# A macaron network of six parts on one Trainium2 core: gate product and integers on VectorE, another order of loads, a signal of their own for ten more scores

## The reference

```python
x = x + 0.5 * ffn8(_ln(x))      # int8 quantised 128x128 product
x = x + enc(_ln(x))             # gated encoder, see below
x = x + 0.5 * ffn8(_ln(x))
x = x + 0.5 * moe(_ln(x))       # top-2 routing to 8 experts, capacity 256, hidden 688
x = x + attn(_ln(x))            # 16 heads of width 8
x = x + 0.5 * moe(_ln(x))       # the same experts again
# in enc: xl = alpha * (dense @ wv + wvb);  sw = sigmoid(-xl) ** 2
#         xo = xl * 2 * sw + 2 * enc * (1 - sw)
# in ffn8: q = clip(round(lhs / scale), -127, 127); acc = q @ q_rhs; acc * scale * rhs_scale
```

## Time and profile before

| | us |
|---|---|
| median of 3 runs (lowest, highest) | 3003.58 (3001.66, 3004.78) |
| the profiled execution | 3014.93 |
| its span | 3012.6 |
| mean granted TensorE clock | 0.852 |

### The profile page before, as it was taken

One profiled execution on the slowest core, in us unless ns is written; L12 is line 12 of the kernel. 1 busy time (PEld: TensorE's weight loads), 2 busy tenths in 40 slices (PEclk: granted clock), 3 DMA queues, 4 the chain that ended last, 5 costly groups with the idle time before them and its releaser, 6 DMA issues.

```text
span 3012.6 us, 42205 instructions
## 1 busy us (share of the span) xinstructions
PE 2171.7 (72%) x13556; PEld 1596.8 (53%) x13556; DVE 1513.2 (50%) x4298; ACT 1242.2 (41%) x2620; POOL 708.3 (24%) x678
## 2 busy tenths in 40 slices
PE   2666662463983888798878888878988898947845
PEld 1454341343752655675666566646755665725734
DVE  4885673333374365457445554564464355345412
ACT  3675203323354345435534553444444334324312
POOL 2110004242122032332134222422232230022042
PEclk9877755685996899999999999999999999969878
DMA  7000000012012121311131213212121311221011
GB/s 219 1 0 0 1 0 5 21 47 48 28 43 47 40 61 43 73 49 50 41 82 56 54 31 75 58 45 56 53 59 44 79 53 44 45 57 52 18 52 37
DMA packets 228506, 140.34 MB, mean 47 GB/s; under 512 B 117073, under 2 KB 206284, under 8 KB 228306
## 3 DMA queue, kind: packets, MB, share of 16 engines
q1 hardware_dynamic: 173264, 84.55, 11.4%
q0 software_dynamic: 16928, 34.72, 4.0%
q10 hardware_dynamic: 38114, 18.53, 2.1%
HBM read 81.50 MB, written 57.15 MB: 46 GB/s over the span
## 4 chain that ended last, share of the span: by engine, by line
PE 49%; DVE 20%; issue 8%; ACT 7%; POOL 5%; DMA 5%; SPq 3%; ACTq 1%; DVEq 1%; POOLq 0%
PE PS L851 15%; PE PS L819 9%; DVE AR L1012 4%; PE PS L1086 4%; PE PS L1123 4%; PE PS L1104 3%; PE PS L1109 2%; DVE small L322 2%; PE PS L1276 2%; POOL AR L701 2%; PE PS L854 1%; DMA OD<-AR 1%; DVE xnT L1184 1%; DMA YE<-AR 1%; SPq L1167 1%
## 5 line engine op out<-in xcount | busy, mean ns | idle before, releaser
L851 PE MATMUL PS<-AR,W 128*128 128x256 f32 x2560 | 649.6, 403 | 18.4 <-DVE AR L747 13.1
L745 DVE TENSOR_TENSOR AR<-AR,PS 128x512 f32<-128x512 f32 (+1 forms) x384 | 229.2, 598 | 757.7 <-ACT AR L786 625.7
L851 PEld LDWEIGHTS PS<-AR,W 128*128 128x128 f32 x2560 | 500.1, 204 | 92.4 <-DVE AR L747 15.3
L1012 DVE TENSOR_REDUCE AR<-PS 128x2 f32<-128x512 f32 x512 | 344.5, 690 | 274.1 <-PE PS L1109 227.3
L786 ACT ACTIVATE AR<-PS 128x512 f32<-128x512 f32 (+1 forms) x384 | 201.5, 526 | 667.4 <-PE PS L851 520.5
L690 POOL DMA_INDIRECT XE<-xn,sidx x256 | 252.2, 985 | 926.6 <-issue 832.2
L1061 ACT ACTIVATE AR<-PS 128x512 f32<-128x512 f32 x512 | 301.6, 599 | 393.3 <-PE PS L1109 389.9
L819 PE MATMUL PS<-AR,WO 128*128 128x256 f32 (+1 forms) x1536 | 378.8, 388 | 0.0
L701 POOL DMA_INDIRECT AR<-YE,gidx x256 | 256.6, 1002 | 361.6 <-DMA YE<-AR 220.9
L819 PEld LDWEIGHTS PS<-AR,WO 128*128 128x128 f32 (+1 forms) x1536 | 281.2, 190 | 77.1 <-issue 42.5
L1086 PE MATMUL PS<-AR 128*128 128x256 bf16 x1024 | 220.1, 302 | 102.2 <-DVE AR L1012 90.4
(11 more groups left out here) (342 smaller groups left out, 2903.1 us busy)
## 6 DMA issues: line engine op xcount, KB each, us to landing
AR<-XE SPq DMA_DIRECT2D x128, 128.0 KB, 2.1
YE<-AR ACTq DMA_DIRECT2D x128, 128.0 KB
AR<-QD SPq DMA_DIRECT2D x384, 32.0 KB
QD<-AR SPq DMA_DIRECT2D x8, 768.0 KB, 5.0
AR<-KD SPq DMA_DIRECT2D x64, 96.0 KB
W<-in_L_ffn_w_kernel_dram SPq DMA_DIRECT2D x2, 2560.0 KB, 13.9
OD<-AR SPq DMA_DIRECT2D x128, 36.0 KB
X<-in_L_attn_dense_dram SPq DMA_DIRECT2D x8, 512.0 KB, 4.4
```

The lines of the kernel that those rows point to most:

```text
L745: ins = dve.tensor_tensor(hf[:, cols], gl[i % 2][:, cols], H[:, 2 * (i % 2) + 1, cols], ALU.mult)
L851: mm = pe.matmul(H[:, b0, b * CAP:(b + 1) * CAP], w[:, e, hb * P:(hb + 1) * P], xeT[e % 2], start=True, stop=True)
L1012: dve.tensor_reduce(mx[c % 2][:, :, b], score_bank(c, b).rearrange("p (h q) -> p h q", h=2), AX.X, ALU.max).then_inc(S["a_mx"], 1)
```

## The change

1. GpSimd's two gate operations go. VectorE adds 2 * enc to x (`encoded`, slot 12), then makes 2 * (xl - enc) * sw and adds it to x (`add`, slot 13 instead of 14). `e_fin`, which frees `xn2`, is now signalled by `encoded`.
2. In these rounds GpSimd's integers go too: VectorE makes them at the end of `quant`, which moves from slot 19 to 18. The LayerNorm before it and all later steps of ffn8 on VectorE, and the matching ones on ScalarE, move one slot ahead. So does the first query pass on ScalarE (`fa[0]`, 16 to 15). The prologue keeps GpSimd's integers.
3. `atail_sp` is put ahead of slot group 3 instead of 2 of SP's list: the load of the third rows stands before its wait and its nine DMAs.
4. `a_s1` is given by the first 18 scores (`SEP = scored(4)`) instead of 8, so VectorE's maxima of scores 8 to 17 wait for the score alone.

```diff
--- before.py
+++ after.py
@@ -395,7 +395,7 @@
         ROUND_Q = (tmp2, SIDE2, qT2, qI2)
 
         def q_dve(dve, n, g, l, rows, where):
-            tmp, side, qT, _ = where
+            tmp, side, qT, qI = where
             ch = Chain(dve, S["q_ch"], n * Q_CH)
 
             def quant():
@@ -406,6 +406,9 @@
                 for t in range(TG):
                     dve.tensor_scalar(tmp[:, t, :], rows[:, t, :], qinv[:, t:t + 1], MAGIC, ALU.mult,
                                       ALU.add).then_inc(S["q_t"], 1)
+                if where is ROUND_Q:
+                    dve.wait_ge(S["q_t"], TG * (n + 1))
+                    dve.tensor_scalar(qI, tmp, MAGIC, QMAX, ALU.subtract, ALU.min).then_inc(S["q_int"], 1)
 
             def turned():
                 dve.wait_ge(S["q_tr"], n + 1)
@@ -500,12 +503,20 @@
                                                  by_parity(xn2, h, v), ALU.mult, ALU.subtract)
                 i.then_inc(S["e_u"], 1)
 
+            def encoded():
+                xg = X[:, bass.ds(g * TG, TG), :]
+                dve.scalar_tensor_tensor(xg, xn2, 2.0, xg, ALU.mult, ALU.add).then_inc(S["e_fin"], 1)
+
             def add():
+                xg = X[:, bass.ds(g * TG, TG), :]
+                dve.wait_ge(S["e_sw"], n + 1)
+                dve.wait_ge(S["e_u"], 2 * n + 2)
+                dve.scalar_tensor_tensor(tmp2, tmp2, 2.0, sg, ALU.mult, ALU.mult).then_inc(S["e_p1"], 1)
+                dve.wait_ge(S["e_p1"], n + 1)
                 dve.wait_ge(S["e_fin"], n + 1)
-                xg = X[:, bass.ds(g * TG, TG), :]
-                dve.scalar_tensor_tensor(xg, tmp2, 2.0, xg, ALU.mult, ALU.add).then_inc(S["x_done"], 1)
-
-            return lambda: gated(0), lambda: gated(1), add
+                dve.tensor_tensor(xg, xg, tmp2, ALU.add).then_inc(S["x_done"], 1)
+
+            return lambda: gated(0), lambda: gated(1), encoded, add
 
         def e_act(act, n):
 
@@ -562,11 +573,6 @@
                 i = pool.tensor_tensor(x4[:, :, v, :], x4[:, :, v, :],
                                        xg0[:, v:v + 1, :].broadcast_to([P, TG // 2, D]), ALU.add)
                 i.then_inc(S["e_enc"] if v else S["e_enc0"], 1)
-            pool.wait_ge(S["e_u"], 2 * n + 2)
-            pool.wait_ge(S["e_sw"], n + 1)
-            pool.tensor_tensor(tmp2, tmp2, sg, ALU.mult).then_inc(S["e_p1"], 1)
-            pool.wait_ge(S["e_p1"], n + 1)
-            pool.tensor_tensor(tmp2, tmp2, xn2, ALU.add).then_inc(S["e_fin"], 1)
 
 
 
@@ -898,6 +904,8 @@
 
             return min(NS, i + PB + 6, PB + 2 * (i + 1))
 
+        SEP = scored(4)
+
         def slot_of(j):
 
             return next(i for i in range(NS) if scored(i) > j)
@@ -1003,8 +1011,8 @@
                                 side_bank(c).rearrange("p (b d) -> p b d", d=AD)).then_inc(S["a_va"], 1)
 
             def maxima(c, b):
-                if c == 0:
-                    dve.wait_ge(S["a_s1"], PB * n + b + 1)
+                if PB * c + b < SEP:
+                    dve.wait_ge(S["a_s1"], SEP * n + PB * c + b + 1)
                 else:
                     dve.wait_ge(S["a_slot"], NS * n + slot_of(PB * c + b) + 1)
                 if b == 0 and c >= 2:
@@ -1795,9 +1803,9 @@
                     lq_ = ln_dve(dve, L_MAIN + R.run(NORMS, "q"), ge)
                     ee = e_dve(dve, ge, ge)
                     qq = q_dve(dve, NG + ge, ge, L_MAIN + R.run(NORMS, "q"), xn2, ROUND_Q)
-                    b.put((0, le[0]), (1, le[1]), (2, le[2]), (9, ee[0]), (10, ee[1]), (14, ee[2]),
-                          (14, lambda: hold(dve, S["x_done"], NG + R.run(UPDATES, "e") + 1)),
-                          (14, lq_[0]), (15, lq_[1]), (16, lq_[2]), (19, qq[0]), (21, qq[1]), (22, qq[2]), (23, qq[3]))
+                    b.put((0, le[0]), (1, le[1]), (2, le[2]), (9, ee[0]), (10, ee[1]), (12, ee[2]), (13, ee[3]),
+                          (13, lambda: hold(dve, S["x_done"], NG + R.run(UPDATES, "e") + 1)),
+                          (13, lq_[0]), (14, lq_[1]), (15, lq_[2]), (18, qq[0]), (20, qq[1]), (21, qq[2]), (22, qq[3]))
                 if R.has(0):
                     g = R.g(0)
                     la = ln_dve(dve, L_MAIN + R.run(NORMS, "a"), g)
@@ -1854,7 +1862,7 @@
                     b.put((5, la[0]))
                     if R.has(1):
                         b.put((7, lambda: hold(act, S["m_scatter0"], 256 * (R.g(1) + 1))))
-                    b.put(*zip((7, 7, 8, 8), la[1:]), (12, ta[0]), (14, ta[1]), (16, fa[0]), (18, fa[1]))
+                    b.put(*zip((7, 7, 8, 8), la[1:]), (12, ta[0]), (14, ta[1]), (15, fa[0]), (18, fa[1]))
                 if R.has(2):
                     ge = R.g(2)
                     le = ln_act(act, L_MAIN + R.run(NORMS, "e"), ge, xn2)
@@ -1864,8 +1872,8 @@
                     if R.has(0):
                         b.put((6, lambda: hold(act, S["m_cmb"], R.run(SUMS, "c0") + 1)))
                     b.put((1, le[0]), *zip((3, 3, 4, 4), le[1:]), (6, te[0]), (7, te[1]),
-                          (11, ee[0]), (12, ee[1]), (12, ee[2]), (15, lq_[0]),
-                          (17, lambda: act.wait_ge(S["e_fin"], ge + 1)), *zip((17, 17, 18, 18), lq_[1:]))
+                          (10, ee[0]), (11, ee[1]), (11, ee[2]), (14, lq_[0]),
+                          (16, lambda: act.wait_ge(S["e_fin"], ge + 1)), *zip((16, 16, 17, 17), lq_[1:]))
                 if R.i == NG:
 
                     b.put((late(4), lambda: hold(act, S["m_scatter1"], 256 * (NG - 1))))
@@ -1967,7 +1975,6 @@
                     gather_pool(pool, 0, 0, 0, 0)
                 if R.has(2):
                     e_pool(pool, R.g(2))
-                    q_pool(pool, NG + R.g(2), ROUND_Q)
                 if R.has(0):
                     afront_pool(pool, R.g(0))
                 if R.i == FIRST:
@@ -1994,7 +2001,7 @@
                 attend_sp(sp, R.g(-1) if R.has(-1) else None, b)
                 b = Beside()
                 if R.has(-1):
-                    b.put((2, lambda: atail_sp(sp, R.g(-1))))
+                    b.put((3, lambda: atail_sp(sp, R.g(-1))))
                 experts_sp(sp, 1, R.heavy("m1", -2), b)
                 if R.has(1):
                     experts_open_sp(sp, 0, R.g(1), R.run(EXPERTS, "m0", -1))
```

## The result

The changed kernel takes 2874.78 us (median of 4 runs, 2865.49 to 2877.91) beside 3003.95 us of the kernel before on the same chip: ratio 0.957, 95% interval 0.954 to 0.959. That is 129 us less, where 115 were forecast. In a later job it was 2877.97 us beside 3007.61, ratio 0.957 (0.955 to 0.958). The profiled execution of the changed kernel was its quickest, 2865.5 us, and that of the kernel before, 3014.9 us, was slower than any of the four timed beside it. I therefore set a second trace of the changed kernel beside it, an execution of 2881 us.

The account below looks back on a forecast made before the run. TensorE's idle time, some 840 us, was what edits could win. Edit 4's 44, edit 3's 14, edits 1 and 2's 25 and 32 gave 115 us off 3014.9: 2899.9, or 2889 us for the median 0.38% lower; range 2861 to 2932.

Parts of the forecast that it names:

- the prediction's second case: Attention's first five slots at the lower clock: TensorE bounds them at 8.7 us, 9.6 with slot 2; gain 4.6 us.
- the gain stays: Behind slot 4 of each attention nothing takes back edit 4's 5.5 us; no further gain was priced there.
- Rival E: Slower than before: TensorE's clock falls because its waits lie between more stretches of half work; 3030 us at 0.80; chance 0.03.
- behind slot 4 every wait is between slots: In each attention, waits after slot 4 are all between slots; given as a reason that edit 4's gain stays.
- The nearest row: L923, a cast of the same size and types, priced VectorE's integers at 0.7 us, bounds 0.7 and 1.4.
- the 9.7 us of the sum: In each of rounds 2 to 5 TensorE gains 3.1 + 6.6 us by the end of the second experts.
- the slack: Third rows of the next first experts arrived 3.2 us before use; added to the list's 5.9 us in rounds 2 to 5.
- A: Attention pairs stay slow: TensorE at the lower clock, a slot's chain not closing in 1.3 us; 2913 us; chance 0.16.
- B: Second experts: integers and neighbouring steps hold VectorE's products; 3 us per round instead of 8; 2909 us; chance 0.12.
- C: SP's list is not late: 12 us per round instead of 8, and 7 us per attention; 2861 us; chance 0.06.
- D: VectorE's integer passes hold GpSimd's scatters and gathers through the port, at most 5.6 us; 2894 us; chance 0.03.
- F: A stage not seen takes all of the gain: within 0.2%, near 3003 us; chance 0.02.

Follow-up runs that it names:

- edit 4 alone: Only the signals for the first 18 scores, on the kernel before: 2959.08 us of 3007.61, ratio 0.984; in the first job ratio 0.994.
- 64 signals: Every one of the 64 scores has its own signal, on the changed kernel with third rows ahead of most key loads: 2801.86 us of 3003.66, ratio 0.932.
- the integers alone: Only the integers moved to VectorE in their old slot, gate still on GpSimd, on the kernel before: 2991.15 us of 3006.40, ratio 0.994.
- Edits 1 and 2 alone: Changed kernel with edits 3 and 4 undone, slot moves kept: 2963.26 us of 3003.66, ratio 0.986; in the first job ratio 0.982.
- the run with the rows ahead: Changed kernel with third rows issued behind the first of four groups of key and query loads: 2827.63 us of 3003.66, ratio 0.941.
- without the moves: Edits 1 and 2 without edits 3 and 4, VectorE's and ScalarE's steps back in their old slots: 2989.56 us of 3006.40, ratio 0.9935.

## Why the prediction was right, and where its sizes were off

**Edit 4: the first five slots right, the clock behind them missed.** Seven of the attentions had 88.0 us in the first five pairs and have 7.3 us each now, 5.3 us less each, and score 8's maximum comes another 0.7 us sooner behind the one before it (21.7 us for 22.3). 5.9 against the 5.5 priced is close. The prediction took VectorE as the bound, 7.4 us with slot 2; it is 7.3. In the eighth, of round 8, where VectorE also runs steps of a LayerNorm between the pairs, the five pairs took 13.7 us before and 9.7 and 11.0 in the two traces, at a clock of 0.72 and 0.50: there the lower level stayed, as in the prediction's second case, 9.6 us. The step that failed is "the gain stays" with a price of nothing behind slot 4: the rest of the first seven attentions took 482 us in the profile before and 476 to 481 in the four other traces without edit 4, but 470 with edit 4 alone and 464 and 470 in the two traces of the changed kernel. That is 1 to 2.6 us for each. It goes with the clock: in rounds 1 to 6 such a stretch takes 66 to 67 us at 1.00 and 70 at 0.90. In the kernel before the clock was low while TensorE idled between half-done pairs. With these gaps gone it was at or near its upper level behind them in most attentions, but 0.90 in one of the seven with edit 4 alone and in one of the second trace. Rival E had the sign wrong: it put the low level down to stretches of half work, which the run of edit 4 alone bears out, but these are what the edit removes. The statement that behind slot 4 every wait is between slots, and so beyond a signal's reach, was wrong too: by the marks 64 signals took 24 us more from the attentions and the first experts ahead of them.

**Edit 3: right in round 2, priced by the wrong row for rounds 6 to 8.** In round 2 slot 3 now starts at 1127.71, released by VectorE, where 41.9 us had been won up to the attention's end: (1172.07 + 0.4) - 1127.71 - 41.9 = 2.9 us, 3.1 forecast. In round 6 VectorE's product of slot 4 (2309.66 before, 2190.86 now) gives 118.8 - 113.8 = 5.0 us, 4.8 forecast, but this agreement is luck. 2.0 of the 5.0 us were there already at slot 0, ahead of the place that edit 3 changes. These are TensorE's first 20 matmuls with weights in the stage, in the kernel before and in the changed one:

```profile
2288.59 6.00 PE L851 MATMUL PS<-AR,W 128*128 128x256 f32 x20
2174.38 4.48 PE L857 MATMUL PS<-AR,W 128*128 128x256 f32 x20
```

The granted clock was 0.57 from 2288 to 2292, and 1.00 in the changed kernel (2174 to 2178). So TensorE came late to the third rows and waited only 4.02 us; it waited 5.8 us in round 6 of the runs of edit 4 alone and of the integers alone, where its start was not late. Nor does edit 3 prevent the late start: the second trace of the changed kernel has it in round 7. Edit 3 has 3.1 us of that mark. The other 2.1 us of that round come in the next first experts, where the wait for third rows fell from 9.72 to 6.69 us, since SyncE's key list moved too; and in rounds 7 and 8 the wait that went was 5.85 and 5.79 us, not the 4.02 of the earlier trace rows. I priced three rounds by the smallest of three rows, one that the clock had cut: 14 for 21 us.

**Edits 1 and 2 without cover: right.** Round -2, VectorE's gate and the integers, against the earlier trace rows:

```profile
467.98 1.22 DVE L514 SCALAR_TENSOR_TENSOR AR<-AR 128x1024 f32<-128x1024 f32 x1 [1.02 <-ACT AR L531]
469.24 1.23 DVE L517 TENSOR_TENSOR X<-X,AR 128x1024 f32<-128x1024 f32 x1
...
480.51 0.69 DVE L411 TENSOR_SCALAR AR<-AR 128x1024 bf16<-128x1024 f32 x1
...
481.26 1.04 PE L445 MATMUL PS<-identb,AR 128*128 128x128 bf16 x8 [17.09 <-DVE AR L411]
```

TensorE's wait fell by 6.8 us in each of rounds -2 and -1 (to 17.09 and 26.72), 6.7 forecast. The third rows of rounds 0 and 1 came 4.8 and 5.9 us sooner, counted from TensorE's first turning of the gate, 5.7 forecast. The nearest row, the cast L923, was the right one for the integers: 0.69 us both. And with GpSimd's pass gone this cast is quick everywhere:

```profile
L931 DVE CAST AR<-xn x8: 693/693/694, 697.2 to 2486.6; 128x1024 bf16<-128x1024 f32 x8
```

**Edits 1 and 2 in the second experts: the right bound, with its sizes off.** TensorE's own gain by the end of the stage was larger than the 9.7 us of the sum. In round 2 it reached the wait for third rows at 1222.21 - 8.19 = 1214.0, 57.0 us ahead of the kernel before, so 15.1 us were won since the attention's end. The integers' idle time went altogether (0.8 was left in the sum), and the 2.50 us at L452, which the sum didn't hold, went too. What goes beyond the list's gain and the slack did not reach the end, because SyncE's list was late, as the prediction had it. The list came 4.1, 4.4, 5.5 and 5.5 us sooner in rounds 2 to 5 (third rows issued at 1219.29, 1483.86, 1746.99 and 2012.12), against 5.9 forecast. And the slack that I had taken from round 2, 3.2 us, was 4.4, 6.6 and 5.2 in rounds 3 to 5 by the same reckoning (issued at 1547.26, 1827.06 and 2112.21, used at 1554.23, 1836.20 and 2119.98). So 19.5 + 19.4 = 38.9 us could be won; the wait behind them shows 8.2, 3.7, 4.4 and 5.6 us, and the marks say 37.6 (34.8 in the second trace). The forecast had 32. Edits 1 and 2 alone brought the list 0.8 us sooner on average, not 2.8; with edit 3 it was 4.9 of 5.9. The slack was read from one round of four, and it was the smallest.

**The rivals.** A is out in seven of the eight attentions, where the pairs' chain closes within VectorE's time; round 8 is the case it describes. B is out for the change, but it is what happens without the moves: 17 us of 40. C, SyncE's list not late, is out by the 8.2 us wait in round 2 and by the run with the rows ahead. Its time of 2861 is as near to the 2875 measured as the forecast's 2889, 14 us each, through the sizes above and not through its mechanism. D: all eight integer passes took 0.694 us, and in this trace GpSimd ran no scatter or gather beside any of them, so what it would have done there no run shows. E and F are out.

## What to carry to other kernels

When a signal at a slot's end is replaced by one at the instruction that matters, count what follows it too: here the clock stayed up for most of the stage, worth 1 to 2.6 us of 69. When several rounds are priced by a row of one of them, take that row from each: twice here the round I had read was the smallest, once because its clock was low. And when an in-order queue is named as the next bound, look at its order before anything is made faster: one load issued ahead of 27 gave 46 us, where both moves to VectorE together gave 40.

## What the runs showed of the hardware

The granted clock was 0.72 and 0.56 in the first five slots of rounds 2 and 3, where VectorE idled 0.94 to 1.56 us in each pair, and 1.00 in both with edit 4 alone, where these gaps are gone. The pass on VectorE and the pass on GpSimd slowed each other before (0.69 to 1.41 us for the cast, 3.64 to 4.42 for the integers); with the one on GpSimd gone, every cast took 0.693. The 27 loads of keys and queries ahead of the third rows took SyncE 10.7 us in round 2 (1208.58 to 1219.29), and with this one load issued before them TensorE's wait of 8.2 us was gone. And the same kernel took 3004 to 3008 us on the three chips of the later jobs and 3332 us on that of the first, where engines stood still for up to 14 us with no releaser in the kernel while GpSimd issued indirect transfers. There the ratios of single edits were no guide: edit 4 had 0.994 for 0.984, and edits 1 and 2 0.982 for 0.986.
